# The last 96 expert blocks reordered, and the sums of four batches put between them

## Chip, cores, metric

The kernel runs on one core of one Trainium2 chip. The metric is the device time of one execution in microseconds. The profiled execution has a span (first to last event in the profile) and a time of its own, which is slightly longer than the span.

## What is computed

The reference is a four-part network over 8 batches of 512 tokens with 256 features: a selective-scan mixer, an attention block with a modulated MLP, gated linear attention, and a mixture of experts. The change touches only the last part. Its arithmetic is:

```
n      = layernorm(x)                                  # x: what the first three parts left
shares, ids = top_k(softmax(n @ router_w.T), 4)        # of 32 experts; shares renormalised
y[k]   = share_k * (silu(n @ gate_w[e_k].T) * (n @ up_w[e_k].T)) @ down_w[e_k].T
out    = x + y[0] + y[1] + y[2] + y[3]                 # for each token
```

There are 4096 tokens and 4 experts for each, so 16384 rows pass through some expert (256 to 96 to 256 features each).

## The kernel before

**Rows by expert.** The first three parts work batch by batch; while they run, GpSimd scatters each batch's normalised tokens by indirect DMA (L1029) into `rows_dram`, a DRAM table with a region for each expert, 4 copies of each token. Next to a token stand three times four columns: where its four copies lie, their shares, and the numbers of the rows of results.

**Blocks.** A block is 128 rows of one expert. A table made on the chip says for each of the NBLK = 160 blocks which expert it has and at which row it begins (128 full blocks and up to 32 for the experts' remainders). The first NBT = 64 blocks are full blocks that exist as soon as six batches are scattered; NBE = 40 of these run in between the earlier work, on other buffers. The remaining blocks, 40 to 159, run at the end in a loop of their own, `experts()`, which each engine has. The table of the 96 late blocks (64 to 159) is made by `block_tables(i)` (L2011 on VectorE, L2662 on TensorE) beside blocks 42, 44, 46 and 48: TensorE counts and sums up over experts by small matmuls with `upto`, `ones_e`, `blocks` and `done_early`; VectorE compares block numbers with the expert's ends. In the order of before the late blocks go expert by expert: all that an expert has left, with rows of all eight batches.

**One step of `experts()`.** Step s works on four blocks at once. TensorE transposes the rows of block s (L2797), multiplies block s-1 by the gate and up weights (L2806), transposes the hidden values of block s-2 (L2817) and multiplies block s-3 by the down weights (L2827). ScalarE copies `xTb` of block s out of PSUM (L1546) and applies Silu to block s-1 (L1552). VectorE makes `h_tok` of block s-1 (L2150), copies `hTb` of block s-2 (L2157) and copies the results y of block s-3 out of PSUM into one of 16 buffers `ys` (L2165). Every fourth step it also finds, for four blocks at a time, to which result row each row belongs (`pick`, L2059, four operations at L2075 to L2082), for which the loaded rows of all four have to be there. GpSimd scatters each y by indirect DMA to `y_dram` (L1108). SyncE loads the rows of a block (`rows_in`, L904, its DMA at L910) into one of 12 buffers as soon as the block that had it is done, and after every eighth late block the residual of one batch (L931).

**Sums.** `y_dram` has four rows for each token. After the last block SyncE waits (`y_gone`, L784) until the last 16 scatters have landed, then reads batch by batch four summands of 128x1024 (512 KB each, L942) into four rotating buffers, and stores a batch's sum (L945). VectorE adds them in four operations of 128x1024 for each batch (L2172 to L2177). SyncE's instructions are executed in order: a wait holds everything behind it.

Of the kernel before, what the change touches and what calls it, by code (L numbers as in the profile page):

```python
# [19 lines left out]
ALU = mybir.AluOpType  # L20
# [4 lines left out]
P = 128  # L25
# [33 lines left out]
NXE = 8  # L59
# [21 lines left out]
TABLES_AT = [NBE + 2 + 2 * i for i in range(4)]  # L81

# [327 lines left out]
def build(nc, counted, x, w, wt, mod_b, wo, g_gk2, g_norm, out):  # L410


    with ExitStack() as ctx:
# [249 lines left out]
        assert at_e[0] <= OFFSET["mod_a"][0]  # L663

# [21 lines left out]
        per_expert = sb("per_expert", 5, parts=EXPERTS)  # L686
# [109 lines left out]
        residual += [nrm, as_tokens(xT.rearrange("p c t -> p (c t)")), as_tokens(hT_all[:, :])]  # L796

# [11 lines left out]
        def _(sp):  # L809
# [105 lines left out]
            def blocks_in():  # L915
# [9 lines left out]
                for b in range(NBT, NBLK):  # L925
                    rows_in(b)


                    c, last_of = divmod(b - NBT, NXS - NYS)
                    if last_of == NXS - NYS - 1 and c < BATCH:  # L930
                        sp.dma_start(residual[c], tokens(x3_dram[c])).then_inc(res_in[c], 16)  # L931

            def sums_io():
                for b in range(NBLK - NYR, NBLK):
                    y_gone(sp, b)
                for c in range(BATCH + 2):
                    if c < BATCH:
                        if c >= NFS:
                            sp.wait_ge(f_sum, c - NFS + 1)
                        for k in range(TOPK):  # L940
                            first = k * TOKENS + c * SEQ
                            sp.dma_start(final[:, c % NFS, k], tokens(y_dram[first:first + SEQ])).then_inc(f_in[c % NFS], 16)  # L942
                    if c >= 2:
                        sp.wait_ge(f_sum, c - 1)
                        sp.dma_start(tokens(out[c - 2]), residual[c - 2]).then_inc(f_out[(c - 2) % NFS], 16)  # L945
# [252 lines left out]
        def _(act):  # L1198
# [341 lines left out]
            def experts():  # L1540
                for s in range(NBE, NBLK + 1):
# [5 lines left out]
                    if s > NBE:  # L1547
# [4 lines left out]
                        a.activation(gated[:, b % 2], bank[2 + b % 2][:, 0:EI], ACT.Silu).then_inc(g_done, 1)  # L1552

# [22 lines left out]
        def _(dve):  # L1576
# [385 lines left out]
            def early_tables():  # L1962


                n, blocks, ends = (per_expert[:, i:i + 1] for i in range(3))
                done, minus = done_early[:, 0:1], done_early[:, 1:2]
# [24 lines left out]
                k.step(d.tensor_scalar(minus, done, -1.0, None, ALU.mult).then_inc(k.sem, 1))  # L1991
                yield
# [18 lines left out]
            def block_tables(i):  # L2011


                n, blocks, ends, left, begins = (per_expert[:, i:i + 1] for i in range(5))
# [3 lines left out]
                if i == 0:  # L2018
# [10 lines left out]
                    k.step(d.tensor_tensor(left, blocks, done_early[:, 0:1], ALU.subtract).then_inc(k.sem, 1))  # L2029
                    marked("tab_blocks", k.n)  # L2030
                if i == 1:
                    k.step(d.tensor_copy(ends, at[0:EXPERTS, 0:1]).then_inc(k.sem, 1))
                    marked("tab_ends", k.n)
                    dve.wait_ge(k.sem, k.n)
                    k.step(d.tensor_tensor(begins, ends, left, ALU.subtract).then_inc(k.sem, 1))
                    k.step(d.tensor_scalar(before_b, block_no[:, 0:NBL], ends, None, ALU.is_ge).then_inc(k.sem, 1))
# [104 lines left out]
            def experts():  # L2141
                for s in range(NBE + 1, NBLK + 4):
# [18 lines left out]
                    if NBE <= b < NBLK:  # L2161
# [748 lines left out]
```

## Time and profile before

| | |
|---|---|
| median of 3 runs | 2917.58 us (2916.7 to 2918.52) |
| profiled execution: time, span | 2919.7 us, 2918.0 us |
| busy: TensorE, VectorE, ScalarE, GpSimd | 83%, 73%, 49%, 22% of the span |
| late blocks alone (block 40 to the last scatter) | about 2662 to 2860 us |
| from the last scatter's landing to the end | 2859.6 to 2918.0 us |

The busy shares are means over stages with different limits, so they say little on this change, which concerns the last tenth of the span. In the rows below, times are us from the span's start unless ns stands there. PEclk is the granted clock of TensorE as a share of 2.4 GHz: 1.00 is 2.4 GHz and 0.50 is 1.2 GHz. The DMA share is the mean busy share of 16 DMA engines.

### The profile page before, as it was taken

The page shows a single profiled execution, that of the slowest core. Times are in us where ns is not written, and L with a number is a line of the kernel's source. Part 1 is how long each engine was busy: PE and PEld are TensorE (multiplying, and loading weights), DVE is VectorE, ACT ScalarE, POOL GpSimd, SP SyncE. Part 2 cuts the span into 40 slices and gives each one's busy share as a digit, 9 for nine tenths or more (in the row PEclk, how much of TensorE's full clock was granted, in tenths as well). Part 3 has the DMA queues.
Part 4 walks back from the last instruction along what each step waited for, and adds up shares of the span by engine and source line. Part 5 has one row for each costly group of instructions (what it writes and reads, how often), then busy time and mean ns, then how long its engine had stood idle before and what let it go on. Part 6 is the DMA issues. An engine that isn't in the chain of part 4 may idle for free.

```text
span 2918.0 us, 37858 instructions
## 1 busy us (share of the span) xinstructions
PE 2434.3 (83%) x12823; PEld 1509.9 (52%) x12823; DVE 2118.6 (73%) x3010; ACT 1419.2 (49%) x2325; POOL 636.6 (22%) x611
## 2 busy tenths in 40 slices
PE   5787798889879888889888888888779897998991
PEld 3764355545544455445544554455435544556880
DVE  3889975898669967896789677976797652246666
ACT  5866345735571556255735563546435326333340
POOL 2002001300240015010320233111500313025661
PEclk8998799969985999699978997899879999978995
DMA  2112220223031312141222211321233174365757
GB/s 105 66 56 99 87 78 9 94 89 112 17 97 60 109 62 83 39 143 63 65 83 95 88 58 53 131 87 30 73 107 100 36 160 162 103 197 153 225 178 306
DMA packets 138314, 288.72 MB, mean 99 GB/s; under 512 B 14208, under 2 KB 83344, under 8 KB 137872
## 3 DMA queue, kind: packets, MB, share of 16 engines
q1 hardware_dynamic: 124304, 247.76, 26.3%
q0 software_dynamic: 13824, 38.55, 3.6%
q8 instruction: 108, 1.77, 0.3%
q14 instruction: 78, 0.64, 0.1%
HBM read 216.72 MB, written 69.54 MB: 98 GB/s over the span
## 4 chain that ended last, share of the span: by engine, by line
PE 50%; DVE 21%; ACT 11%; issue 8%; POOL 6%; DMA 2%; SPq 1%; DVEq 0%; POOLq 0%; ACTq 0%; PEldq 0%
PE bank L2257 10%; DVE scan L1690 5%; PE bank L2516 5%; PE bank L2270 4%; PE bank L2455 4%; PE bank L2471 3%; PE bank L2435 3%; PE bank L2806 3%; DVE rest L1846 3%; ACT rest L1433 2%; PE bank L2244 2%; PE bank L2542 2%; DVE scan L1699 2%; PE bank L2827 2%; DVE scan L1686 2%
## 5 line engine op out<-in xcount | busy, mean ns | idle before, releaser
L1690 DVE TENSOR_TENSOR_SCAN scan<-scan 128x1024 f32<-128x1024 f32 x224 | 516.3, 2305 | 46.2 <-ACT scan L1389 40.7
L1389 ACT ACTIVATE scan<-scan 128x511 f32<-128x511 f32 x512 | 339.4, 714 | 384.1 <-DVE scan L1690 366.4
L2435 PE MATMUL bank<-ident,scan 128*128 128x128 f32 x2048 | 306.3, 303 | 85.4 <-DVE scan L1699 77.2
L2435 PEld LDWEIGHTS bank<-ident,scan 128*128 128x128 f32 x2048 | 261.0, 157 | 149.8 <-DVE scan L1699 79.1
L1699 DVE TENSOR_TENSOR scan<-scan 128x1024 f32<-128x1024 f32 x256 | 320.4, 1252 | 5.0 <-DVE rest L1881 1.0
L2516 PE MATMUL bank<-rest 32*128 32x384 f32 (+3 forms) x1024 | 268.1, 636 | 50.8 <-DVE rest L1846 37.4
L1714 DVE TENSOR_TENSOR scan<-scan 128x1024 f32<-128x1024 f32 x224 | 277.7, 1240 | 9.7 <-PE bank L2435 5.0
L1029 POOL DMA_INDIRECT rows_dram<-stage,slot_at x128 | 177.7, 1388 | 461.9 <-DVE chosen L1793 345.3
L1007 POOL TENSOR_SCALAR rs<-mv 128x4 f32<-128x4 f32 x24 | 21.1, 878 | 1087.6 <-DVE off L1601 1086.9
L1846 DVE TENSOR_REDUCE rest<-bank 128x2 f32<-128x1024 f32 (+3 forms) x176 | 195.7, 1123 | 49.6 <-PE bank L2521 47.9
L1433 ACT ACTIVATE rest<-bank 128x2048 f32<-128x2048 f32 (+3 forms) x128 | 158.3, 1237 | 140.6 <-PE bank L2542 140.4
L2257 PE MATMUL bank<-scan 128*128 128x512 f32 x320 | 169.6, 662 | 27.4 <-DVE xa L1662 19.6
L2257 PE MATMUL bank<-xT,scan 128*128 128x512 f32 x320 | 147.4, 612 | 7.8 <-ACT xT L1401 7.7
L1881 DVE TENSOR_TENSOR rest<-rest,bank 128x512 f32<-128x512 f32 x64 | 43.9, 685 | 148.6 <-PE bank L2257 95.0
L2516 PEld LDWEIGHTS bank<-rest 32*128 32x128 f32 x1024 | 98.6, 239 | 95.3 <-DVE rest L1846 52.9
L1108 POOL DMA_INDIRECT y_dram<-rest,y_at x120 | 115.0, 959 | 58.2 <-DVE rest L2165 43.2
L2455 PE MATMUL bank<-wslot,rest 128*128 128x256 f32 x512 | 120.1, 380 | 1.9 <-DVEq L1884 1.9
L2471 PE MATMUL bank<-hT,wslot 128*128 128x512 f32 x256 | 120.0, 595 | 1.9 <-DVE rest L1871 1.9
L2257 PE MATMUL bank<-hT,wslot 128*128 128x512 f32 x256 | 119.7, 604 | 0.0
L2270 PE MATMUL bank<-scan,xT 128*128 128x256 f32 x512 | 118.5, 384 | 1.4 <-ACT xT L1216 1.4
L2270 PE MATMUL bank<-scan 128*128 128x160 f32 (+1 forms) x512 | 107.1, 372 | 14.8 <-ACT scan L1302 7.4
L2542 PE MATMUL bank<-rest 32*128 32x512 f32 (+3 forms) x1024 | 115.7, 524 | 0.0
(399 smaller groups left out, 4439.8 us busy)
## 6 DMA issues: line engine op xcount, KB each, us to landing
scan<-bc_dram SPq DMA_DIRECT2D x240, 512.0 KB, 3.8
wslot<-wt SPq DMA_DIRECT2D x64, 384.0 KB, 3.1
rows_dram<-scan SPq DMA_DIRECT2D x32, 670.0 KB, 4.1
scan<-y_dram SPq DMA_DIRECT2D x32, 512.0 KB, 10.0
rest<-rows_dram SPq DMA_DIRECT2D x108, 134.0 KB, 2.8
scan<-rows_dram SPq DMA_DIRECT2D x52, 134.0 KB, 3.2
scan<-wt SPq DMA_DIRECT2D x4, 1536.0 KB, 15.9
wslot<-x SPq DMA_DIRECT2D x8, 512.0 KB, 3.7
```

The lines of the kernel that those rows point to most:

```text
L1389: i = a.activation(decay[:, unit % 2, n, 1:], dt[:, c, 1:], ACT.Exp, scale=a_neg[:, c, 2 * pair + n:2 * pair + n + 1])
L1433: a.activation(probT[:, u % NPT, :, 0:SEQ - j * P], banks(("ST", u))[:, :, 0:SEQ - j * P], ACT.Exp)\
L1690: d.tensor_tensor_scan(flat, decay[:, unit % 2].rearrange("p n t -> p (n t)"), flat, 0.0, ALU.mult, ALU.add).then_inc(decay_used.sem, 1)
L1699: d.tensor_tensor(drive[:, unit % NDRIVE], drive[:, unit % NDRIVE], bc[:, load % 2, 1], ALU.mult).then_inc(unit_done.sem, 1)
L1714: d.tensor_tensor(drive[:, unit % NDRIVE], dtu[:, c].unsqueeze(1).broadcast_to([P, 2, SEQ]), bc[:, load % 2, 0], ALU.mult).then_inc(drive_ ...
L1846: d.tensor_reduce(nmax[:, t, heads, r].rearrange("p i r -> p r i"), banks(("S", u))[:, :, 0:n * width].rearrange("p r (i k) -> p r i k", i=n),
L2257: m = t_.matmul(b[0:rows, cols], lhsT, rhs, start=(i == 0), stop=(i == len(pairs) - 1))
L2270: m = t_.matmul(b[:, j * 256:j * 256 + width], src[c][:, t * P:(t + 1) * P], weights[:, c], start=(c == 0), stop=(c == parts - 1))
L2435: m = t_.matmul(A.bank(("yT", c))[:, t * P:(t + 1) * P], drive[:, unit % NDRIVE, n, t * P:(t + 1) * P], ident[:, :], is_transpose=True, st ...
L2455: m = t_.matmul(D[t // 2][:, (t % 2) * HID:(t % 2 + 1) * HID], inner[:, f % 2, t * P:(t + 1) * P], slot[:, 2 * NF * P:], start=(first and ...
L2471: t_.matmul(b[:, :], lhsT, rhs, start=(i == 0), stop=False, skip_group_check=True)
L2516: t_.matmul(b[:, k, at:at + width], qT[rows, i, t * P:(t + 1) * P], kT[rows, i, 0:width], start=(i == heads.start), stop=False, skip_group ...
```

## The change

Three edits go together.

- **Order of late blocks.** An expert's rows of the first six batches come first in its region. The table now lists, for all experts, first the blocks that hold any of these (`held6` of them, counted in the early tables), then, for all experts, the blocks that are left. So every row of batches 0 to 5 lies in a block below NB6 = 96 + 31 = 127. The number of blocks stays 160.
- **Sums between the last blocks.** SyncE reads the summands of batches 0, 1 and 2 after it has issued the row loads of blocks 142, 146 and 156 (before the first it waits until the scatters of blocks 111 to 126 have landed), those of 3, 4 and 5 after the last row load, each after the sum of two batches before has been stored, and those of 6 and 7 after the last scatter has landed. VectorE does the sums of batches 0 to 3 in the steps 141 to 144, 145 to 148, 152 to 155 and 157 to 160, one addition at the end of a step; those of 4 to 7 follow the loop. Summands of batches 0 to 5 go into two sets of buffers outside the weights in use.
- **Late results.** From block 64 on, ScalarE copies y out of PSUM, one step later than VectorE did.

The diff, cut to its core:

```diff
+NB6 = (BATCH - 2) * SEQ * TOPK // P + EXPERTS - 1
+Y_BY_ACT = NBT
+SUM_READS = {NB6 + 15: 0, NB6 + 19: 1, NB6 + 29: 2}
+SUMS_AT = {NB6 + first + i: (c, i) for c, first in enumerate((14, 18, 25, 30)) for i in range(4)}
+NASIDE = BATCH - 2
...
@@ SyncE, blocks_in, after rows_in(b)
+                    if b in SUM_READS:
+                        if SUM_READS[b] == 0:
+                            for done in range(NB6 - NYR, NB6):
+                                y_gone(sp, done)
+                        if SUM_READS[b] >= 2:
+                            sum_out(SUM_READS[b] - 2)
+                        sum_in(SUM_READS[b])
+
+            def sum_in(c):
+                for k in range(TOPK):
+                    first = k * TOKENS + c * SEQ
+                    sp.dma_start(summand(c, k), tokens(y_dram[first:first + SEQ])).then_inc(f_in[c % NFS], 16)
+
+            def sum_out(c):
+                sp.wait_ge(f_sum, c + 1)
+                sp.dma_start(tokens(out[c]), residual[c]).then_inc(f_out[c % NFS], 16)
 
             def sums_io():
+                for c in range(len(SUM_READS), NASIDE):
+                    sum_out(c - 2)
+                    sum_in(c)
                 for b in range(NBLK - NYR, NBLK):
                     y_gone(sp, b)
-                for c in range(BATCH + 2):
...
+                for c in range(NASIDE, BATCH):
+                    sum_in(c)
+                for c in range(NASIDE - 2, BATCH):
+                    sum_out(c)
...
@@ ScalarE, experts, behind Silu
+                    b = s - 4
+                    if Y_BY_ACT <= b < NBLK:
+                        act.wait_ge(y_ready, b + 1)
+                        act.wait_ge(y_copied, b)
+                        y_gone(act, b - NYR)
+                        a.activation(ys[:, (b - NBE) % NYR], bank[6 + b % 2][:, 0:HID], ACT.Copy).then_inc(y_copied, 1)
...
@@ VectorE, block_tables
-                    k.step(d.tensor_tensor(left, blocks, done_early[:, 0:1], ALU.subtract).then_inc(k.sem, 1))
+                    k.step(d.tensor_tensor(left, held6, done_early[:, 0:1], ALU.subtract).then_inc(k.sem, 1))
+                    k.step(d.tensor_tensor(left_c, blocks, held6, ALU.subtract).then_inc(k.sem, 1))
...
+                    k.step(d.tensor_scalar(before_c, block_no[:, 0:NBL], ends_c, None, ALU.is_ge).then_inc(k.sem, 1))
...
+                    k.step(d.tensor_scalar(begun_c, block_no[:, 0:NBL], begins_c, None, ALU.is_ge).then_inc(k.sem, 1))
...
@@ VectorE, experts, end of step s
-                    if NBE <= b < NBLK:
+                    if NBE <= b < Y_BY_ACT:
                         dve.wait_ge(y_ready, b + 1)
...
+                    if s in SUMS_AT:
+                        sum_step(*SUMS_AT[s])
+
+            def sum_step(c, i):
+                part = [summand(c, k) for k in range(TOPK)]
+                if i == 0:
+                    dve.wait_ge(f_in[c % NFS], 16 * TOPK * (c // NFS + 1))
+                    d.tensor_tensor(part[0], part[0], part[1], ALU.add).then_inc(f_pair, 1)
+                if i == 1:
+                    d.tensor_tensor(part[2], part[2], part[3], ALU.add).then_inc(f_pair, 1)
+                if i == 2:
+                    dve.wait_ge(res_in[c], 16)
+                    dve.wait_ge(f_pair, 3 * c + 1)
+                    d.tensor_tensor(residual[c], residual[c], part[0], ALU.add).then_inc(f_pair, 1)
+                if i == 3:
+                    dve.wait_ge(f_pair, 3 * c + 3)
+                    d.tensor_tensor(residual[c], residual[c], part[2], ALU.add).then_inc(f_sum, 1)
 
             def sums():
-                for c in range(BATCH):
...
+                for c in range(len(SUMS_AT) // 4, BATCH):
+                    for i in range(4):
+                        sum_step(c, i)
...
@@ TensorE, block_tables
-                    t_.matmul(at[0:EXPERTS, 0:1], upto[:, :], left, start=True, stop=True).then_inc(tab_pe, 1)
+                    t_.matmul(at[0:EXPERTS, 0:1], upto[:, :], left, start=True, stop=True)
+                    t_.matmul(at[0:EXPERTS, 1:2], upto[:, :], left_c, start=True, stop=False)
+                    t_.matmul(at[0:EXPERTS, 1:2], every, left, start=False, stop=True).then_inc(tab_pe, 1)
...
-                    t_.matmul(at[0:1, 256:256 + NBL], blocks, before_b, start=True, stop=False)
-                    t_.matmul(at[0:1, 256:256 + NBL], done_early[:, 1:2], begun_b, start=False, stop=True).then_inc(tab_pe, 1)
+                    t_.matmul(at[0:1, 256:256 + NBL], held6, before_b, start=True, stop=False)
+                    t_.matmul(at[0:1, 256:256 + NBL], done_early[:, 1:2], begun_b, start=False, stop=False)
+                    t_.matmul(at[0:1, 256:256 + NBL], blocks, before_c, start=False, stop=False)
+                    t_.matmul(at[0:1, 256:256 + NBL], minus6, begun_c, start=False, stop=True).then_inc(tab_pe, 1)
```

## Rows read from the trace of the kernel before

**Rows 1.** Windows of 5 us: busy us of each engine, PEclk, DMA share, GB/s

```profile
2630.00:2635.00 5.00, 3.54 (x23) 2.67 (x22) 3.30 (x12) 2.06 (x6) 1.93 (x2) 1.00 0.23 77
...
2660.00:2665.00 5.00, 2.54 (x8) 1.94 (x9) 4.45 (x18) 1.55 (x3) 0.06 (x1) 0.50 0.46 115
...
2815.00:2820.00 5.00, 5.00 (x31) 4.17 (x30) 3.63 (x15) 2.12 (x7) 2.95 (x4) 1.00 0.51 163
...
2895.00:2900.00 5.00, 0.00 (x0) 0.00 (x0) 3.42 (x4) 0.00 (x0) 0.00 (x0) 0.50 1.02 413
```

**Rows 2.** Groups by form, 2700 to 2850 (busy us, mean ns, idle before)

```profile
L1108 POOL DMA_INDIRECT y_dram<-rest,y_at x103 | 98.7, 958 | 53.0 <-DVE rest L2165 42.6 <-issue 10.4
...
L2165 DVE COPY rest<-bank 128x256 f32<-128x256 f32 x96 | 39.6, 413 | 1.2 <-PE bank L2827 0.9
L1546 ACT ACTIVATE rest<-bank 128x256 f32<-128x256 f32 x96 | 36.8, 383 | 64.0 <-PE bank L2797 62.6 <-issue 1.3
...
L2150 DVE SCALAR_TENSOR_TENSOR rest<-rest,scan,bank 128x96 f32<-128x96 f32 x95 | 29.9, 314 | 48.3 <-ACT rest L1552 47.4
```

**Rows 3.** Timeline of a block step: start, us, engine, line

```profile
2804.53 0.17 DVE L2075 TENSOR_TENSOR scan<-rest,scan 128x16 f32<-128x16 f32 x1
...
2805.38 0.32 DVE L2150 SCALAR_TENSOR_TENSOR rest<-rest,scan,bank 128x96 f32<-128x96 f32 x1
2805.48 0.38 PE L2797 MATMUL bank<-ident,rest 128*128 128x128 f32 x2
...
2805.61 0.28 DVE L2157 COPY rest<-bank 96x128 f32<-96x128 f32 x1
```

**Rows 4.** Timeline, 2848 to 2918

```profile
2850.37 0.38 PE L2797 MATMUL bank<-ident,rest 128*128 128x128 f32 x2
...
2857.14 0.96 POOL L1108 DMA_INDIRECT y_dram<-rest,y_at  x1 [0.30 <-issue]
2859.59 7.07 SPq L942 DMA_DIRECT2D scan<-y_dram  x12
2868.02 1.23 DVE L2172 TENSOR_TENSOR scan<-scan 128x1024 f32<-128x1024 f32 x1 [12.75 <-DMA scan<-y_dram]
...
2910.11 1.23 DVE L2172 TENSOR_TENSOR scan<-scan 128x1024 f32<-128x1024 f32 x1 [1.59 <-DMA scan<-y_dram]
...
2914.89 0.33 SPq L945 DMA_DIRECT2D out<-hT  x1
```

**Rows 5.** DMA issues, 2655 to 2918: count, KB each, median us to landing

```profile
rest<-rows_dram SPq DMA_DIRECT2D x108, 134.0 KB, 2.8
...
out<-scan SPq DMA_DIRECT2D x3, 512.0 KB, 8.1
...
out<-hT SPq DMA_DIRECT2D x1, 512.0 KB, 2.6
```

**Rows 6.** Timeline of SyncE's DMA issues, merged

```profile
2687.15 8.53 SPq L910 DMA_DIRECT2D rest<-rows_dram  x8
...
2786.68 47.29 SPq L910 DMA_DIRECT2D rest<-rows_dram  x32
```

**Rows 7.** Timeline of the late tables on VectorE and TensorE

```profile
2673.58 0.25 DVE L2036 TENSOR_SCALAR scan<-block_no,per_expert 32x96 f32<-32x96 f32 x1
...
2677.88 0.20 DVE L2050 TENSOR_SCALAR scan<-scan 1x96 int32<-1x96 f32 x1
...
2676.21 0.32 PE L2673 MATMUL bank<-scan,ones_e 32*1 32x96 f32 x2
```

**Rows 8.** Timeline of VectorE and GpSimd in the scan stage

```profile
1670.01 1.22 DVE L1699 TENSOR_TENSOR scan<-scan 128x1024 f32<-128x1024 f32 x1
...
1670.04 2.01 POOL L1029 DMA_INDIRECT rows_dram<-stage,slot_at  x1 [0.31 <-issue]
```

**Rows 9.** Timeline of TensorE, first late blocks

```profile
2663.59 1.65 PE L2806 MATMUL bank<-scan,rest 128*128 x4
...
2670.26 0.81 PE L2806 MATMUL bank<-scan,rest 128*128 x4
```

More of the change, by code:

```diff
@@ L663, in build @@
         assert at_e[0] <= OFFSET["mod_a"][0]
+        before_c, begun_c = (whole[0:EXPERTS, GU + i * NBL:GU + (i + 1) * NBL] for i in range(2))
+        every = chunk_starts[0:EXPERTS, 1:1 + EXPERTS]
         xTb, gated, h_tok = pass_buffer(HID, 2), pass_buffer(EI, 2), pass_buffer(EI, 2)
@@ L796, in build, with summand @@
         residual += [nrm, as_tokens(xT.rearrange("p c t -> p (c t)")), as_tokens(hT_all[:, :])]
+        slice_at = [GU + i * NT * HID for i in range(3)] + [at_e[0] + i * NT * HID for i in range(2)]
+        assert slice_at[2] + NT * HID <= OFFSET["wq"][0] + NXE * ROW and slice_at[4] + NT * HID <= RES
+        assert at[0] + NT * HID <= 20 * SEQ + 16
+        slices = [as_tokens(whole[:, i:i + NT * HID]) for i in slice_at] + [xa, xb, as_tokens(R[:, at[0]:at[0] + NT * HID])]
+        def summand(c, k):
+            return slices[c % 2 * TOPK + k] if c < NASIDE else final[:, c - NASIDE, k]
         passed = sem("passed")
@@ L1540, in experts @@
             def experts():
-                for s in range(NBE, NBLK + 1):
+                for s in range(NBE, NBLK + 4):
                     if s < NBLK:
@@ L1965, in early_tables @@
                 n, blocks, ends = (per_expert[:, i:i + 1] for i in range(3))
+                held6 = per_expert[:, 5:6]
                 done, minus = done_early[:, 0:1], done_early[:, 1:2]
@@ L1991, in early_tables @@
                 k.step(d.tensor_scalar(minus, done, -1.0, None, ALU.mult).then_inc(k.sem, 1))
+                k.step(d.tensor_scalar(more, block_no[:, 0:EXPERTS], float(P), None, ALU.mult).then_inc(k.sem, 1))
+                dve.wait_ge(k.sem, k.n)
+                k.step(d.tensor_scalar(more, more, n, None, ALU.is_lt).then_inc(k.sem, 1))
+                dve.wait_ge(k.sem, k.n)
+                k.step(d.tensor_reduce(held6, more, AX.X, ALU.add).then_inc(k.sem, 1))
                 yield
@@ L2011, in block_tables @@
             def block_tables(i):
-                n, blocks, ends, left, begins = (per_expert[:, i:i + 1] for i in range(5))
+                n, blocks, ends, left, begins, held6, left_c, ends_c, begins_c, minus6, wrap = (per_expert[:, i:i + 1] for i in range(11))
                 at = bank[5]
@@ L2026, in block_tables @@
                     dve.wait_ge(k.sem, k.n)
-                    k.step(d.tensor_tensor(left, blocks, done_early[:, 0:1], ALU.subtract).then_inc(k.sem, 1))
+                    k.step(d.tensor_tensor(left, held6, done_early[:, 0:1], ALU.subtract).then_inc(k.sem, 1))
+                    k.step(d.tensor_tensor(left_c, blocks, held6, ALU.subtract).then_inc(k.sem, 1))
                     marked("tab_blocks", k.n)
+                    k.step(d.tensor_scalar(minus6, held6, -1.0, None, ALU.mult).then_inc(k.sem, 1))
+                    k.step(d.tensor_scalar(wrap, ident[0:EXPERTS, EXPERTS - 1:EXPERTS], -float(EXPERTS), 1.0, ALU.mult, ALU.add).then_inc(k.sem, 1))
                 if i == 1:
                     k.step(d.tensor_copy(ends, at[0:EXPERTS, 0:1]).then_inc(k.sem, 1))
+                    k.step(d.tensor_copy(ends_c, at[0:EXPERTS, 1:2]).then_inc(k.sem, 1))
                     marked("tab_ends", k.n)
@@ L2662, in block_tables @@
             def block_tables(i):
-                n, blocks, ends, left = (per_expert[:, i:i + 1] for i in range(4))
+                n, blocks, ends, left, begins, held6, left_c, ends_c, begins_c, minus6, wrap = (per_expert[:, i:i + 1] for i in range(11))
                 at = bank[5]
```

26 lines of the change are left out of this document (5 added, 21 removed).

## Prediction, made before the changed kernel had run

> **What bounds the kernel now.** The windows of 5 us come first. In the late part of the span TensorE is busy 5.00 of 5 us at a granted clock of 1.00, so there the matmuls of the expert blocks set the pace; from 2860 on TensorE does nothing, VectorE is partly idle, and the DMA engines are full (share 1.02, 413 GB/s) [rows 1]. These are two stages with two limits. Second, the groups by form of 2700 to 2850 show that in the block stage DVE's y copy (L2165, 413 ns) hardly waits, GpSimd's scatter (L1108) costs 958 ns and waits another 0.51 us each, and `h_tok` (L2150) sits idle 0.5 us per block waiting for ScalarE: VectorE and GpSimd have slack, TensorE has none [rows 2]. Third, the timeline of single steps gives the pace: block 130 is transposed at 2805.48 and block 159 at 2850.37, so a block costs 44.89 / 29 = 1.548 us [rows 3, 4]. Fourth, the timeline of the tail: the last scatter starts at 2857.14; SyncE, which waits for it, issues the first read of sums at 2859.59 (so a scatter lands 2.45 us after it starts); the first sum starts 8.43 us later, at 2868.02; the last sum starts at 2910.11 and the span ends 7.89 us after that [rows 4]. Between first and last, seven batches pass in 42.09 us, 6.01 each; a batch moves 2.10 MB in and 0.52 MB out, which at 413 GB/s is 6.3 us. So the last 58 us are a DMA-bound stage in which TensorE does nothing, after a TensorE-bound stage in which the DMA share is 0.51 [rows 1]. Moving reads from the one to the other is where time can come from.
>
> **The tail after the change.** Batches 0 to 5 have all their rows in blocks below 127 (96 full blocks and 31 for the remainders), so their sums may start before the last block. Behind the last scatter stay only the reads of batches 6 and 7, their sums, and the last stores. From the rows of the tail: first set 8.43, second set 2.10 MB / 413 GB/s = 5.1 (no store stands between them now), from the last sum's start to the end 7.89. If the last scatter landed at 2859.59 as before, the span would end at 2859.59 + 8.4 + 5.1 + 7.9 = 2881.0. The same end comes out of the queue: batch 5's reads are issued after batch 3's sum, about step 160 (2854.7), behind batch 4's; they are done by about 2863, two sets at 5.1 follow until 2873, and 7.9 gives 2881. The two paths tie, so whatever delays the block stage counts in full. Without losses that is 37 us less. The losses:
>
> *Tables (L2011, L2662).* About ten small VectorE operations and four matmul pairs more, in steps 42 to 48, and three operations in the sixth batch's tables. Nearest rows: a 32x96 comparison 0.25 us, three such matmul pairs 0.32 us each on overlapping starts [rows 7]. Two comparisons, four tiny operations and three matmul pairs stand on the chain through block 46: 0.4 + 0.3 + 0.5 = 1.2; the steps have some slack, I take 1.0 (0 if it is absorbed, 2.5 if all of it stands on TensorE's path). SyncE does not wait longer for it: its late loads start at 2687.15 [rows 6], and the last table row is ready at 2677.88 [rows 7].
>
> *The y copy moves to ScalarE.* VectorE loses 413 ns a block, ScalarE gains the same copy, 128x256 out of PSUM, which costs it 383 ns in L1546 [rows 2]; that row shows 64.0 us of idle over 96 blocks, 0.67 us each, ahead of the next copy, so it fits. TensorE waits for neither, so nothing is won. GpSimd gets each y about a step later, which only shifts it. Cost 0 (up to 0.2 per block, 1.5 in all, if the copy crosses the next `xTb`).
>
> *The sums between blocks.* One sum operation is a 1024-column addition; in the tail four start within 4.9 us (1.22 each). A VectorE step after the change is `h_tok` and `hTb`, which start 0.23 us apart and take 0.31 and 0.28, about 0.43 together, and a `pick` every fourth step of 0.85 (2804.53 to 2805.38) [rows 3]. A sum of four steps needs 4 x (0.43 + 1.22) + 0.85 = 7.45 us against 4 x 1.548 = 6.19 from TensorE. Batches 0 and 1 stand back to back (steps 141 to 148): 2.5 us over. Batches 2 and 3 stand alone, 1.25 over, of which half a step's slack hides 0.5: 0.75 each. Together 4.0. Bounds: 0 if TensorE's lead of a step hides it, 16 x 1.22 = 19.5 if every addition falls on the path.
>
> *Row loads behind the reads.* SyncE first waits for the scatter of block 126: its copy comes at about 2807.2 in step 130, plus 2.45 and a small queue, 2810.2. Four reads then take it about 1.9 us to issue, and every row load 8.53 / 8 = 1.07 [rows 6]. SyncE runs 11 blocks ahead of TensorE: it issues block 159's load at about 2833.6, while 159 is transposed at 2850.37 [rows 4, 6]; that is 17 us of lead. The store of batch 0, issued when later reads are already queued, took 8.1 us to land in the median of its kind, the last one, alone, 2.6 [rows 5]: what is issued later on this queue waits. So the load of block 143 lands after batch 0's reads, about 2820.5 (2.10 MB at some 328 GB/s, an estimate: 413 less the scatters' 0.13 MB per 1.548 us; and latency); `pick` of 140 to 143 needs it at 2823.1. Block 147, behind batch 1's reads too, lands at about 2830 and is needed at 2829.3 plus the delay of the sums, about 2831. So margins of 2.6 and 1 us: I take 1.0 for this (0 to 11; the far end if reads get only the 0.49 of the DMA share that was free, 200 GB/s, so that a set takes 10.5 us and not 6.4).
>
> On that queue the row just read is 8.1 against 2.6 us. The Trainium skill, DMA: Bandwidth & Descriptors, section Queues, rings and completion order, says that each engine consumes the descriptors of one ring in ring order; the trace agrees. If instead a row load kept its median of 2.8 us [rows 5] whatever stood ahead of it, this term would be 0 and not 1.0.
>
> *GpSimd beside the sums.* In the scan stage a scatter which started 0.03 us after a 1024-column VectorE addition took 2.01 us and not 0.96, that is, it ended 0.96 after the addition did [rows 8]. In a step with a sum that can add up to 1.05 to a scatter, which hides under GpSimd's idle time as long as it is one block a step; only the last blocks, beside the sums of batches 3 and 4, delay the final landing: 1.0 (0 to 8.4, eight scatters).
>
> The Trainium skill, SBUF — State Buffer, section Who interferes with whom, infers that a tensor_tensor holds only the read side of the port shared with GpSimd and so doesn't stall descriptor generation. This trace speaks against it: by the page this term would be 0, by the row it is 1.0.
>
> **Sum.** 2881.0 + 1.0 + 0 + 4.0 + 1.0 + 1.0 = 2888.0 us of span. The profiled execution of before is 2919.7 with a span of 2918.0, 1.7 more; its median of runs is 2917.58, 2.1 less than that execution. So 2888.0 + 1.7 - 2.1 = **2887.6 us**, 30 us or 1.0% less.
>
> **The rivals.** *Nothing is lost* (losses under 3 us): TensorE's lead absorbs additions and loads; for it, half a microsecond of VectorE idle per block [rows 2] and a DMA share of 0.51; against it, 7.45 against 6.19 us. 2881 to 2884. *Row loads starve the blocks*: reads at 200 GB/s, 11 us for 1 in the sum: 2897.6. For it, loads that queue; against it, 11 blocks of lead. *Additions don't overlap*: 19.5 for 4.0: 2903. Against it, TensorE can do the results and next two products of a step while VectorE adds. *GpSimd falls behind*: 8.4 for 1.0: 2895. *The change doesn't do what it says*: early reads or sums wait in effect until the last block, as the in-order SyncE is held; the tail stays, 2917 or so. *Slower*: starving TensorE loses it its clock. At a granted clock of 0.50, as in 2660 to 2665 [rows 1], four gate matmuls took 1.65 us against 0.81 at full clock [rows 9], so a block would cost about 3.0 us, 1.5 more. From the first late load (step 133) to the end, 29 blocks, that is 43 us: 2931. It decides from some 20 slow blocks on, since 30 us are to be given back. Against it: in 2630 to 2635 TensorE was busy only 3.54 of 5 us and the clock stayed 1.00 [rows 1]; 6.19 of 7.45 us is busier than that.
>
> **How the numbers follow.** Forecast (losses 3 to 10 us, 2884 to 2891): 0.52. Nothing lost 0.18, loads starve 0.12, additions don't overlap 0.07, GpSimd behind 0.06, no effect 0.02, slower 0.03. The range 2880 to 2900 holds the first three and GpSimd's case, some 0.85. About 0.2% (5.8 us) is what a measurement of this kernel can tell from no change; by the cases, faster 0.95, same 0.02, slower 0.03.
>
> **What the changed profile would show.** Right: DMA share near 1 between about 2811 and 2873; only eight reads after the last scatter; the first sum on VectorE near 2823; steps 141 to 148 about 1.85 us apart, and a span near 2888. Wrong: `pick` idle on a row load for more than 2 us (starved); scatters of 2 us in a row, and SyncE waiting long after the last matmul (GpSimd); a granted clock below 1.00 between 2811 and 2860; or TensorE's last matmul later than about 2865, which would put the losses above 10 us.

## The result and the profile after

The changed kernel takes 2894.6 us in the median of 5 runs (2887.05 to 2897.68), the kernel before 2917.58 us beside it (5 runs, 2911.01 to 2929.59). The ratio is 0.9913, with a 95% interval of 0.9884 to 0.9941: 23 us less, where 30 were forecast. The time lies in the range, the sign is right, and the forecast is 7.0 us too low.

The profiled execution of the changed kernel took 2887.05 us (span 2885.1), the shortest of its five. That it nearly equals the forecast is chance: the stages ahead of the change ended 11.6 us earlier in it. Block 40 is transposed at 2650.70 us here and at 2662.32 before, and between the 14 profiled executions of this study that moment wanders from 2649.0 to 2662.3. So everything below is counted from block 40's first transpose. From there to the end, called the late stage, the kernel before needs 255.7 us, the changed one 234.4, and the forecast was 2888.0 - 2662.3 = 225.7. To explain are 21.3 us gained, and 8.7 that were forecast and did not come.

The timeline of the changed kernel (start, us, engine, line, operation) holds the ends of these stages: the weight loads of the first transposes of blocks 40 (2650.70) and 159 (2845.98), SyncE's first read of sums, the longest scatter, the first read of batch 5, the last scatter, SyncE's next read, the first additions of batches 5, 6 and 7, the last addition and the last store.

```profile
2650.70 0.29 PEld L2864 LDWEIGHTS bank<-ident,scan 128*128 128x128 f32 x2 [3.87 <-issue]
...
2802.68 1.79 SPq L963 DMA_DIRECT2D scan<-y_dram  x4
...
2826.93 2.81 POOL L1141 DMA_INDIRECT y_dram<-rest,y_at  x1 [0.30 <-ACT rest L1591]
...
2845.98 0.36 PEld L2864 LDWEIGHTS bank<-ident,rest 128*128 128x128 f32 x2
...
2852.31 0.43 SPq L963 DMA_DIRECT2D scan<-y_dram  x1
...
2855.58 0.96 POOL L1141 DMA_INDIRECT y_dram<-rest,y_at  x1 [0.30 <-issue]
...
2862.71 4.29 SPq L963 DMA_DIRECT2D scan<-y_dram  x8
2864.18 1.23 DVE L2225 TENSOR_TENSOR scan<-scan,xa 128x1024 f32<-128x1024 f32 x1 [4.95 <-DMA rest<-y_dram]
...
2870.75 1.23 DVE L2225 TENSOR_TENSOR scan<-scan 128x1024 f32<-128x1024 f32 x1 [1.82 <-DMA scan<-y_dram]
2877.27 1.23 DVE L2225 TENSOR_TENSOR scan<-scan 128x1024 f32<-128x1024 f32 x1 [1.76 <-DMA scan<-y_dram]
...
2880.80 1.23 DVE L2234 TENSOR_TENSOR hT<-hT,scan 128x1024 f32<-128x1024 f32 x1
2882.06 0.33 SPq L967 DMA_DIRECT2D out<-hT  x1
```

Compared with [rows 4], eight reads instead of 32 stand behind the last scatter. But that scatter starts 9.60 us after block 159's transposes (6.98 before), and SyncE goes on 7.13 us after its start (2.45 before). From SyncE's first read to the end pass 2885.1 - 2802.68 = 82.4 us.

The windows of the changed kernel (columns as in [rows 1]):

```profile
2795.00:2800.00 5.00, 5.00 (x29) 3.85 (x28) 2.28 (x10) 2.73 (x9) 2.60 (x4) 1.00 0.48 155
2800.00:2805.00 5.00, 5.00 (x29) 3.87 (x28) 2.28 (x10) 2.73 (x9) 2.83 (x4) 1.00 0.58 177
2805.00:2810.00 5.00, 5.00 (x32) 4.25 (x30) 1.93 (x8) 3.09 (x10) 3.17 (x4) 1.00 1.01 365
...
2845.00:2850.00 5.00, 4.70 (x22) 2.96 (x20) 3.99 (x7) 2.14 (x8) 3.29 (x3) 1.00 0.98 377
...
2855.00:2860.00 5.00, 0.00 (x0) 0.00 (x0) 4.20 (x4) 0.00 (x0) 1.24 (x2) 0.50 0.99 299
2860.00:2865.00 5.00, 0.00 (x0) 0.00 (x0) 0.82 (x1) 0.00 (x0) 0.00 (x0) 0.50 0.74 283
...
2805.00:2880.00 75.00, 45.59 (x245) 34.96 (x243) 52.24 (x110) 25.32 (x83) 38.98 (x31) 0.82 0.97 357
```

The change does what it says: from 2805 on the DMA engines are full (0.97 in the mean of 75 us) while TensorE still computes at a granted clock of 1.00. They move 357 GB/s in that stretch, not the 413 of [rows 1].

The groups by form of 2690 to 2840, as in [rows 2]:

```profile
L1141 POOL DMA_INDIRECT y_dram<-rest,y_at x97 | 99.8, 1029 | 50.9 <-ACT rest L1591 40.0 <-issue 10.3 <-DVE rest L2217 0.6
...
L1579 ACT ACTIVATE rest<-bank 128x256 f32<-128x256 f32 x91 | 35.0, 384 | 43.1 <-PE bank L2864 42.4 <-issue 0.7
L1591 ACT ACTIVATE rest<-bank 128x256 f32<-128x256 f32 x87 | 32.9, 378 | 0.1
L2202 DVE SCALAR_TENSOR_TENSOR rest<-rest,scan,bank 128x96 f32<-128x96 f32 x92 | 28.9, 314 | 72.0 <-ACT rest L1585 71.3 <-PE bank L2884 0.5
...
L2884 PEld LDWEIGHTS bank<-ident,rest 128*96 128x96 f32 x91 | 11.3, 124 | 9.3 <-issue 5.5 <-DVE rest L2202 1.2
```

The y copy costs ScalarE 378 ns and fits, with 43 us of idle time left ahead of `xTb`; `h_tok` waits longer (72.0 against 48.3 us). Neither looks like a loss. Yet blocks 64 to 141, ahead of any addition and nearly all ahead of any read, take 125.2 us instead of 121.3.

All profiled executions, counted in the same way (us; a block's moment is its first transpose's weight load; "scatter" is the last scatter's start, "next read" SyncE's next read after it). Each row is a single execution; the two of the changed kernel differ by 2.1 us in blocks 64 to 141 and in the late stage.

| kernel | blocks 40-64 | 64-141 | 141-159 | 159 to scatter | scatter to next read | first read to end | late stage |
|---|---|---|---|---|---|---|---|
| before | 38.64 | 121.30 | 27.90 | 6.98 | 2.45 | 58.4 | 255.7 |
| e1 order and tables only | 39.92 | 120.34 | 27.85 | 7.00 | 2.46 | 59.1 | 256.6 |
| e2 ScalarE's copy only | 39.24 | 124.18 | 29.89 | 7.70 | 2.45 | 58.8 | 262.2 |
| e5 VectorE's copy a step later | 40.37 | 120.86 | 27.96 | 8.58 | 2.46 | 58.4 | 258.7 |
| changed | 39.48 | 125.23 | 30.57 | 9.60 | 7.13 | 82.4 | 234.4 |
| e11 changed, again | 39.74 | 123.11 | 30.70 | 8.41 | 7.73 | 82.2 | 232.3 |
| e3 ScalarE's copy from 127 on | 39.49 | 121.08 | 30.52 | 8.38 | 6.65 | 81.9 | 229.4 |
| e4 no copy on ScalarE | 40.50 | 121.05 | 35.14 | 9.92 | 6.75 | 88.5 | 237.0 |
| e6 additions cut | 39.29 | 125.70 | 30.32 | 7.54 | 5.55 | 78.9 | 231.1 |
| e7 batch 5's reads held | 39.86 | 124.20 | 30.45 | 9.55 | 3.03 | 81.8 | 233.6 |
| e8 e3, additions in halves | 39.33 | 120.75 | 31.71 | 8.56 | 8.21 | 84.1 | 231.3 |
| e9 register read moved | 41.14 | 121.47 | 32.67 | 8.39 | 6.62 | 82.6 | 233.1 |
| e10 e3, last sums one by one | 39.96 | 120.19 | 30.83 | 8.34 | 7.01 | 80.3 | 227.4 |
| e12 scatters held | 39.77 | 124.99 | 33.16 | 12.32 | 5.38 | 85.2 | 237.9 |

### The profile page after: what moved, and what is told of

Its sections match the earlier page's. It is cut to its first block and busy times, and to the rows that moved or that the text cites. A ratio compares the mean times of both kernels' runs of the same rounds, so it can differ in the third digit from the quotient of the medians.

```text
span 2885.1 us, 37896 instructions
## 1 busy us (share of the span) xinstructions
PE 2426.8 (84%) x12833; PEld 1498.9 (52%) x12833; DVE 2085.9 (72%) x2924; ACT 1446.4 (50%) x2421; POOL 643.4 (22%) x611
## 5 line engine op out<-in xcount | busy, mean ns | idle before, releaser
L1141 POOL DMA_INDIRECT y_dram<-rest,y_at x120 | 124.5, 1038 | 58.8 <-ACT rest L1591 41.5
L2319 PEld LDWEIGHTS bank<-scan 128*128 128x128 f32 x320 | 62.7, 210 | 102.9 <-issue 52.0
```

The source lines that it names most:

```text
L1141: g.indirect_dma_start(y_dram, bass.IndirectOffsetOnAxis(ap=y_at[:, b % NYA:b % NYA + 1], axis=0), y[:, n % y.shape[1]], None).then_inc(y_ ...
L2319: m = t_.matmul(b[0:rows, cols], lhsT, rhs, start=(i == 0), stop=(i == len(pairs) - 1))
```

## The experiments

### e1 to e4: which part slows the blocks

e1 is the kernel before with the new order of blocks and its tables alone; e2 is the kernel before with ScalarE copying y and nothing else; e3 and e4 are the changed kernel with one constant changed.

```diff
-Y_BY_ACT = NBT
+Y_BY_ACT = NB6     # e3: from block 127 on
+Y_BY_ACT = NBLK    # e4: never
```

> The kernel before with the new order of the late blocks and its longer tables alone; sums and the y copy as before. Measure: from the transposes of block 64 to those of block 141 (before 121.3 us, changed kernel 125.2), and from block 40 to block 64 (38.6 and 39.5). Theory A, ScalarE's y copy slows each block: 121.3 +- 0.8 here. Theory B, the order of the blocks or the tables slow them: about 125. Theory C, a chance difference of one execution: anything between 120 and 126 with no pattern over the four runs. By all three the tables cost about 0.8 us up to block 64, and the tail from the last scatter's landing to the end stays 58.4 us. Whole time by A: about 1 us more than before.

> The kernel before with the y copy of blocks 64 to 159 on ScalarE, one step later, alone. Theory A: 64 to 141 in about 125 us, and some 5 us more over all 96 blocks, so about 0.2% slower than before. Theory B: 121.3 and no change of the time. Theory C: no pattern.

> The changed kernel with ScalarE copying y only from block 127 on (VectorE does 64 to 126). Theory A: block 64 to 126 in about 98.1 us as before (changed kernel 100.7), and the end about 2.5 us earlier than the changed kernel, provided VectorE's relief is wanted only beside the sums. Theory B: no difference from the changed kernel.

> The changed kernel with all y copies on VectorE. Theory A: 64 to 141 in about 121.3 us. Then a step with a sum costs VectorE 0.41 us more: a sum of four steps 4 x (0.43 + 0.41 + 1.22) + 0.85 = 9.1 us against 6.2 from TensorE, so blocks 141 to 159 take about 10 us longer than before (changed kernel: 2.7 longer), and the end comes about 3 us later than in the changed kernel (4 won, 7 lost). Theory B: 125 and the end about 7 us later.

Measured: e1 0.9997 of the kernel before (0.9983 to 1.0011), e2 1.0035 (1.0015 to 1.0054), e3 0.9916 (0.99 to 0.9932), e4 0.9927 (0.9911 to 0.9942). In the table, 64 to 141 takes 123.1 to 125.7 us in all six executions in which ScalarE copies these blocks' y at the changed kernel's place (e9 stands apart, below), and 120.2 to 121.3 in all seven in which it doesn't. So it is neither chance nor the new order: the copy on ScalarE costs 2.9 us alone (e2) and 3.8 between the means of the two groups, in a stretch where it wins nothing. And e4 shows what it is for: with y on VectorE beside the additions, blocks 141 to 159 take 35.1 us and not 30.6 (7.2 more than before, where 10 were expected). Since neither e1 nor e2 wins anything, the 21.3 us come from the edit that is left, the sums between the blocks.

### e5: is it that the copy comes a step later?

The kernel before, with VectorE's copy moved from step b + 3 to b + 4.

```diff
-                for s in range(NBE + 1, NBLK + 4):
+                for s in range(NBE + 1, NBLK + 5):
...
-                    b = s - 3
+                    b = s - 4
```

> The kernel before, with VectorE still copying y, but one step later (as late as the copy on ScalarE is in the changed kernel). If ScalarE's own work is what slows the blocks, the stretch from block 64 to block 141 stays as in the kernel before, 121.3 us or less by 1, and 141 to 159 stays at 27.9. If the later copy is what slows them (the two y banks come free later, TensorE waits for them), the stretch is 124 to 125 us, as in the run that only moved the copy to ScalarE (124.2), and 141 to 159 about 29.9.

Measured: 120.86 and 27.96 us. Lateness doesn't slow these blocks; ScalarE's copy does. The last scatter, however, starts 1.60 us later after block 159 by the lateness alone (8.58 against 6.98).

### e9: where TensorE loses the time

Two neighbouring steps of the changed kernel, a long and a short one, in the timeline of weight loads:

```profile
2734.39 0.36 PEld L2864 LDWEIGHTS bank<-ident,rest 128*128 128x128 f32 x2
2734.72 0.62 PEld L2873 LDWEIGHTS bank<-scan,rest 128*128 128x128 f32 x4
2735.76 0.12 PEld L2884 LDWEIGHTS bank<-ident,rest 128*96 128x96 f32 x1 [0.42 <-issue]
2736.02 0.30 PEld L2894 LDWEIGHTS bank<-scan,rest 96*128 96x128 f32 x2
2736.35 0.36 PEld L2864 LDWEIGHTS bank<-ident,rest 128*128 128x128 f32 x2
2736.68 0.62 PEld L2873 LDWEIGHTS bank<-scan,rest 128*128 128x128 f32 x4
2737.34 0.12 PEld L2884 LDWEIGHTS bank<-ident,rest 128*96 128x96 f32 x1
```

The long step (1.96 us) differs from the short one (1.58) in one place: the load for the `h_tok` transpose comes 1.37 us after the step's first load, and not 0.99, and the profile names no engine that it waits for ("issue"). `h_tok` had been written by 2734.60. Over blocks 64 to 140 this interval is 0.92 us at the least; it is over 1.1 in 4 to 7 of 77 steps without ScalarE's copy and in 13 to 22 with it, and what follows it is 0.59 in both. Between the gate matmuls and this transpose the program has `choose(s + 1)`, which reads the next block's expert number from the on-chip table into a register of TensorE's sequencer. e9 moves it:

```diff
                         m.then_inc(g_ready, 1)
-                    if NBE < s + 1 < NBLK and s + 1 != NBT:
-                        choose(s + 1)
...
                         t_.matmul(bank[6 + b % 2][:, 0:HID], hTb[0:EI, b % 2], weights, ...)
+                    if NBE < s + 1 < NBLK and s + 1 != NBT:
+                        choose(s + 1)
```

> The changed kernel, with the read of the next block's expert number into a register (choose(s + 1)) moved from between a step's gate matmuls and its transpose of h_tok to behind its result matmuls. In the changed kernel the whole difference between long and short steps lies between a step's first transpose and the weight load of the h_tok transpose: 0.92 us at the least, 1.04 in the mean of blocks 64 to 140 (0.99 before); what follows is 0.59 us in both. If TensorE's sequencer waits there for this register read, the stretch before the h_tok transpose shrinks to 0.92 to 0.95 in nearly all steps, and the wait, if any is left, shows ahead of the next step's transposes: 64 to 141 between 119 us (read hidden) and 127 (less cover behind the result matmuls than behind the four gate matmuls). If it is something else at that place (a semaphore of the h_tok or y copies), the long steps stay where they are: 17 or so of them, 1.04 us in the mean, 64 to 141 at 124 to 126.

Measured: 64 to 141 in 121.47 us, with ScalarE copying every y. The interval ahead of the `h_tok` transpose falls to 0.87 us in the mean, over 1.1 in no step, and the wait is now ahead of the step's first transposes. The waits of TensorE's weight loads in 2700 to 2790 (engine, tile, line, released by: us in total, times, longest), e9 first, then the changed kernel:

```profile
PEld bank L2864 <- issue: 14.3, 57, 0.5
PEld bank L2873 <- issue: 0.4, 2, 0.2
```

```profile
PEld bank L2884 <- issue: 3.1, 12, 0.4
PEld bank L2894 <- issue: 1.2, 6, 0.3
```

So the wait moves with the register read: that read is what TensorE's sequencer stands at. Behind the four gate matmuls most of it is covered; behind the result matmuls a wait shows in all 57 steps, 0.25 us in the mean and 0.5 at the most.

### e12: is it the scatter beside the register read?

Why ScalarE's copy makes the read longer is a further question. With the copy on ScalarE, GpSimd's scatters start 0.2 to 0.7 us into a step and not at 1.1, that is, beside the read. e12 was to shift them back.

```diff
                     pool.wait_ge(y_copied, b + 1)
+                    if b >= Y_BY_ACT:
+                        pool.wait_ge(x_copied, min(b + 6, NBLK))
```

> The changed kernel, with GpSimd's scatter of a late block held until ScalarE has copied the xTb of the step after the one in which y was copied, so that it starts about 1.1 us after a step's first transpose, where it starts in most steps of the kernel before, and not at 0.2 to 0.7, where it starts in some 60 of 77 steps of the changed kernel. Theory: the scatter's start beside TensorE's register read is what makes that read long. In the changed kernel 13 of 61 steps with a scatter in that interval are long (over 1.1 us to the h_tok transpose), in the kernel before 3 of 58 with a scatter between 0.7 and 1.3. Then 4 to 7 of 77 steps are long and blocks 64 to 141 take 120.2 to 121.5 us, though ScalarE still copies every y. Rival: it is ScalarE's copy itself, wherever the scatter starts: 12 to 22 long steps, and 123 to 125.7 us. The scatters aren't slower for it; the last one is held by nothing more, and the ratio to the kernel before is 0.990 to 0.992 if the theory holds, 0.991 to 0.994 if not.

A step is called long where more than 1.1 us pass ahead of its `h_tok` transpose. The shift missed its place: the scatters started some 0.8 us after the copy that they waited for, 58 of them between 0.0 and 0.3 us into a step and only 7 between 0.9 and 1.3. 17 of 77 steps are long, 64 to 141 takes 124.99 us, and the ratio is 0.9935 (0.9917 to 0.9953). So this run can't decide as it was meant to. What speaks against the theory is a count over the other timelines: of steps with a scatter that starts at 0.2 to 0.7 us, 5 of 100 are long in the seven kernels without ScalarE's copy and some 64 of 306 in five with it; at 0.7 to 1.3, 16 of 378 and 13 of 53. At the same phase ScalarE's copy still makes the difference. How it lengthens the register read stays open.

e12 also shows what an addition's wait can do. Its timeline in step 154, 4.67 us long:

```profile
2841.93 1.23 DVE L2227 TENSOR_TENSOR scan<-scan 128x1024 f32<-128x1024 f32 x1 [2.88 <-DMA scan<-y_dram]
...
2843.92 0.32 DVE L2204 SCALAR_TENSOR_TENSOR rest<-rest,scan,bank 128x96 f32<-128x96 f32 x1
...
2844.28 0.12 PEld L2886 LDWEIGHTS bank<-ident,rest 128*96 128x96 f32 x1 [3.10 <-DVE rest L2204]
```

VectorE stood 2.88 us at an addition whose summands hadn't landed; the `h_tok` queued behind it came late, and TensorE waited 3.10 us.

### e6: the additions cut

The additions between blocks (batches 0 to 3) are cut to one of 256 features of each token; reads, waits and stores stay.

```diff
+                total = residual[c]
+                if c < len(SUMS_AT) // 4:
+                    part, total = [p[:, :, 0:1] for p in part], total[:, :, 0:1]
```

> The changed kernel, with the additions between blocks (batches 0 to 3) cut to one feature of each token; the other 255 features of these four sums are left out. Reads, stores and waits stay. If the 1024-column additions slow GpSimd's scatters, the scatters between 2800 and 2856 go back to 0.96 us, none over 1.2, and the last scatter starts 7.0 us after block 159's transposes (9.6 in the changed kernel, 7.0 before). If the additions also cost TensorE, blocks 141 to 159 take 28 to 29 us instead of 30.6; if the row loads or ScalarE's copy do that, they stay at 30 to 30.6. If the late landing of the last scatter comes from the queued reads alone, it stays about 7 us (last scatter's start to SyncE's next read); if it comes from scatters that are backed up, it goes back to about 2.5.

Measured (one run): 2881.9 us. No scatter is over 1.05 us, where the changed kernel has 15 after 2710 (1.25 to 2.81), and the last starts 7.54 us after block 159 instead of 9.60. So the 1024-column additions do lengthen the scatters. But blocks 141 to 159 stay at 30.32 us, beside 30.45 to 30.70 in three executions with the additions (changed, e7, e11): the additions' own time costs TensorE next to nothing. Of the 2.67 that these blocks lose, e2 shows 1.99 without any sum. The rest goes with waits for reads, as in e6's own step 154:

```profile
2835.45 0.17 DVE L2228 TENSOR_TENSOR scan<-scan 128x4 f32<-128x4 f32 x1 [1.64 <-DMA scan<-y_dram]
...
2837.08 0.13 PEld L2887 LDWEIGHTS bank<-ident,rest 128*96 128x96 f32 x1 [0.89 <-DVE rest L2202]
```

The last scatter still takes 5.55 us to release SyncE, which lies between the two cases that were expected.

### e7: batch 5's reads held until the last scatter has landed

```diff
-                for c in range(len(SUM_READS), NASIDE):
+                for c in range(len(SUM_READS), NASIDE - 1):
                     sum_out(c - 2)
                     sum_in(c)
+                sum_out(NASIDE - 3)
...
-                for c in range(NASIDE, BATCH):
+                for c in range(NASIDE - 1, BATCH):
```

> The changed kernel, with the reads of batch 5 issued only after the last scatter has landed. If the queued reads of batches 4 and 5 hold up the last scatter's descriptors, the time from its start to SyncE's next read falls from 7.1 us to 2.5 to 3.5, and then three sets follow instead of two: about 8.0 + 6.5 + 6.5 + 7.8 from that read to the end, so that the late stage (block 40 to the end) is about 236, 1.5 over the changed kernel's 234.4. If the reads aren't what delays it, it stays near 7 and the late stage is about 241.

The timeline of e7 around its last scatter:

```profile
2863.22 0.96 POOL L1142 DMA_INDIRECT y_dram<-rest,y_at  x1 [0.30 <-issue]
...
2866.25 0.32 SPq L963 DMA_DIRECT2D scan<-y_dram  x1
```

The landing takes 3.03 us and not 7.13. So reads already queued by SyncE hold up a scatter that GpSimd issues later, on another queue. But nothing is won: from the first read to the end it is 81.8 us, as in the changed kernel, since batch 5's reads now stand behind the landing. The 4.7 us of late landing were no loss of their own; the DMA engines carried batch 5's reads in them.

### e8: additions in halves, on top of e3

```diff
+                halves = [slice(0, NT // 2), slice(NT // 2, NT)] if c < len(SUMS_AT) // 4 else [slice(0, NT)]
...
+                for h in halves:
+                    d.tensor_tensor(to[:, h], to[:, h], by[:, h], ALU.add).then_inc(...)
```

> The changed kernel, with ScalarE copying y only from block 127 on, as in the run before with that edit (late stage 229.4 us, last scatter 8.4 us after block 159's transposes), and each addition between blocks in two halves of 512 columns. If a scatter waits until the VectorE addition that has begun is done, it waits at most 0.65 us and not 1.2: scatters beside additions take about 1.5 us, the last scatter comes 7.5 to 8 us after block 159, and the late stage is 1 us shorter, 228.5. If the scatters are delayed by the sum of VectorE's work and not by the length of one instruction, they take 2 us as before, and the 16 additional instructions make blocks 141 to 159 up to 1 us longer: late stage 230.4. Ratio to the kernel before 0.990 to 0.992 in both cases.

Measured: 0.991 (0.9894 to 0.9927), late stage 231.3 against e3's 229.4. The scatters beside the first two sums are no shorter (1.32 to 2.94 us), the last one comes 8.56 us after block 159 (8.38 in e3), and blocks 141 to 159 take 1.2 us longer. The length of one instruction isn't what delays a scatter; that theory falls.

### e10 and e11: a better version, beside the changed kernel

e10 is e3 with the last batch's summands added to the residual one by one as they land (four semaphores `f_last` in place of one count).

```diff
+                if c == BATCH - 1:
+                    dve.wait_ge(f_last[i], 16)
...
+                    d.tensor_tensor(residual[c], residual[c], part[i], ALU.add).then_inc(f_sum if i == 3 else f_pair, 1)
+                    return
```

> A version meant to beat the changed kernel: ScalarE copies y only from block 127 on (late stage 229.4 us with that alone), and the last batch's four summands are added to the residual one by one, each as soon as it has landed, so that one addition of 1.2 us stands behind the last read and not four (4.8 us). If the end hangs on that chain, the late stage is 3.0 to 3.6 us shorter, 226 to 226.5, and the time is 0.9% to 1.1% below the kernel before by some 28 to 31 us. If the last read itself comes later because the DMA engines are full to the end, nothing or less than 1 us is won: late stage 228.5 to 229.5.

> The changed kernel itself once more, on the same chip as the two others, so that they can be compared. By its first runs: ratio 0.9913 (0.9884 to 0.9941) to the kernel before; late stage 234.4 us, blocks 64 to 141 in 125.2, if that profile was typical; a late stage below 231 or a stretch below 122.5 would mean that the slow blocks were chance.

Measured on the same chip: e10 2883.05 us, 0.9898 of the kernel before (0.988 to 0.9916); e11 2891.72, 0.9928 (0.9906 to 0.995). e10 is the best kernel of the study, 8.7 us below the changed one by the medians, though the two intervals overlap a little. By the late stages it is 4.9 us, 232.3 against 227.4, of which e3's edit is 2.9 and the last sums 2.0, not the 3.0 to 3.6 expected; as two executions of one kernel differ by 2.1, this split is not firm. The end of e10 in the timeline shows what now stands there:

```profile
2872.43 1.23 DVE L2243 TENSOR_TENSOR xT<-xT,scan 128x1024 f32<-128x1024 f32 x1
2873.57 1.22 DVE L2230 TENSOR_TENSOR hT<-hT,scan 128x1024 f32<-128x1024 f32 x1
2875.25 3.89 DVE L2230 TENSOR_TENSOR hT<-hT,scan 128x1024 f32<-128x1024 f32 x3 [0.46 <-DVE hT L2230]
...
2879.16 0.33 SPq L968 DMA_DIRECT2D out<-hT  x1
```

The last three additions run back to back, 1.30 us each, and the profile puts their waits down to the addition before, not to reads: the chain of four dependent additions has become the end.

## Why the prediction was right in sign and 7 us too low

The 8.7 us of the late stage split at SyncE's first read of sums. The forecast had it at 2810.2 - 2662.3 = 147.9 us after block 40, and 77.8 us from there to the end. It came at 152.0 and took 82.4: 4.1 us late (2.6 by slower blocks 64 to 126, 0.8 by blocks 40 to 64, which that moment left out), 4.6 us long. Along the forecast's other path, through the last scatter, 1.4 of the 8.7 arise up to block 159, 6.3 from there to SyncE's next read (4.7 of it the late landing) and 1.0 behind it. Taking the late landing away didn't move the end (e7), so neither path alone holds the 8.7.

**Reads out of the tail: right.** The stretch behind the last scatter shrank as forecast in kind, the DMA share is near 1 from 2805 on, and the granted clock stayed 1.00 while blocks ran, so that "slower by a low clock" falls. "Nothing lost" and "no effect" fall too.

**Tables, 1.0: it fits, but isn't shown.** Blocks 40 to 64 took 0.84 us longer, in e1 1.28. But e2 and e5, which have the old tables, took 0.60 and 1.73 longer (e5 with a later copy there), so single executions can't tell it.

**The y copy on ScalarE, 0 and at most 1.5: the step that failed.** It said "TensorE waits for neither, so nothing is won", and costed the copy at nothing because it fits into ScalarE's idle time. It fits, and it still costs: e2, the copy alone, loses 2.9 us in blocks 64 to 141 and 2.0 in 141 to 159. In the changed kernel blocks 64 to 141 lose 3.9 (2.6 ahead of the first read; in e11 1.8 and 1.1), and e3 wins these back. The place is TensorE's register read (e9); the way from the copy to the read is open.

**Sums between blocks, 4.0, and row loads, 1.0: together too high.** Blocks 141 to 159 lost 2.67 us, 1.99 of them by the copy if that is as in e2; 0.7 are left for both. Steps 141 to 148 came 1.6 us apart in the mean (1.54 before), not 1.85. The forecast's 7.45 us for four steps are 1.86 for one. Beside blocks an addition starts 1.56 us after the one before (four of batch 0 in 4.67 us), all else of the step included, and that is nearly TensorE's pace. Among the waits of 2800 to 2886 no weight load of TensorE is listed with a row load; the rival "loads starve" falls. What did cost was another wait, the additions' for their own summands, with `h_tok` behind them.

**GpSimd beside the sums, 1.0: the mechanism is right, the size isn't settled.** The last scatter came 2.6 us later after block 159 (1.4 in e11). Without any addition between blocks it came 0.6 to 1.6 later (e6, e2, e5), which goes with the copy a step later. Against e6 the additions make 2.1 of it, or 0.9 by e11. The scatters take 1.25 to 2.81 us beside them and 0.96 without. One sign of being wrong showed here: SyncE's next read came 9.6 us after TensorE's last matmul, 4.8 before. The Trainium skill, SBUF — State Buffer, section Who interferes with whom, infers that a tensor_tensor doesn't stall descriptor generation; here the measurement decides against it, by the scatters beside additions (up to 2.81 us) and by e6 without them (none over 1.05).

**The DMA-bound stretch: mis-sized.** The forecast let the reads pass at 413 GB/s, a window of [rows 1], and let batch 5's be done before the last eight were issued, so that "the two paths tie". That window was not far from the mean of the old tail, the last stretch of the kernel before (columns as in [rows 1]):

```profile
2860.00:2912.00 52.00, 0.00 (x0) 0.00 (x0) 34.96 (x30) 0.00 (x0) 0.00 (x0) 0.50 0.99 393
```

The new stretch doesn't reach it: 75 us from 2805 on pass at 357 GB/s. That is 26.8 MB, for which 413 would have needed 64.8 us and 393 would have needed 68.2. The second set took 6.5 us, not 5.1. The forecast said that "no store stands between them now", but the stores of batches 4 and 5 were issued at 2867.04 and 2868.96, beside it, and in the old tail the last five sets, each with a store beside it, took 6.3 to 6.4. A full DMA queue would also explain why the unpriced late landing (7.13 for 2.45) cost nothing in e7, and why first read to end is 81.8 to 82.4 us in four executions (changed, e3, e7, e11) that differ in blocks, scatters and landing. It isn't DMA alone: without the additions it is 78.9, at 375 GB/s (e6), and with y on VectorE beside the additions 88.5 (e4). What the cause of the lower rate is (scatters and row loads in the mix, reads mixed with stores, gaps such as the 0.74 of 2860 to 2865) was not tried. Scatters and row loads aren't all of it: the three windows from 2865 to 2880, with neither left, have 403, 325 and 356 GB/s.

On the landing, the row is 7.13 us with batch 5's reads queued against 3.03 in e7, where all earlier reads had landed (the last at 2854.91). The Trainium skill, DMA: Bandwidth & Descriptors, section Queues, rings and completion order, says that each DMA engine takes turns between queues packet by packet; the changed kernel's trace agrees that another queue's transfer is slowed, not blocked: SyncE went on at 2862.71, after three of batch 5's four reads had landed and before the fourth (2864.15).

**Two readings that don't hold.** The scatter of [rows 8] ended 0.82 us after the addition beside it (1672.05 against 1671.23), not 0.96. And from step 133 to the last block there are 27 blocks, not 29, which makes the rival "slower" about 2928 and not 2931. Neither changes the forecast.

## What to carry to other kernels

Work that moves under another stage is paid at the rate of that stage: the old tail's 393 GB/s in the mean were not reached in the new mix of transfers, 357 were, so a rate that is carried over needs a margin. An engine with idle time is no proof that a copy on it is free; give it the copy only where its old engine needs the room (e3, one constant away, is 3 to 5 us better in its late stage than the two executions of the changed kernel, though its ratio, 0.9916, can't be told from their 0.9913 and 0.9928). Before a wait goes into an in-order engine between blocks, look at what is queued behind it: here `h_tok`, and with it TensorE.

## What was not expected of the hardware

- A read of one number from on-chip memory into a register of TensorE's sequencer costs up to 0.45 us of TensorE's time per step behind 0.81 us of matmuls (changed kernel), and it gets longer more often when ScalarE copies 128x256 out of PSUM in the same step (long reads in 13 to 22 of 77 steps against 4 to 7). Neither the copy's lateness nor, by the counts, the scatter's phase explains it.
- An addition of 1024 columns on VectorE stretches an indirect scatter from 0.96 to as much as 2.81 us, and halving the addition doesn't shorten that (2.94).
- A scatter's landing goes from 2.45 to 7.13 us behind reads that another queue issued 1.3 to 3.3 us earlier; without these it takes 3.03 (e7).
